# A quantised feed-forward stage: rows turned by transposing DMAs, a third double bank, two scalings on ScalarE

## The chip, the cores and the metric

The kernel runs on one core of a Trainium2 chip. The metric is device time in microseconds (us) for one execution of the whole program, and less is better. The times and the profile are of one core throughout.

## The reference, cut to what matters

One decoder layer on 16 sequences of 256 tokens and 512 features: a state-space block, a cross attention block and a feed-forward block, each followed by a layer normalisation without weights. Only the last block is touched:

```python
def _quant_weight(w):                      # ternary weights
    scale = jnp.clip(jnp.mean(jnp.abs(w)), EPS, None)
    wq = jnp.clip(jnp.round(w / scale), -1.0, 1.0) * scale
def _quant_act(x):                         # 8 bits, one scale for each row
    scale = 127.0 / jnp.clip(jnp.max(jnp.abs(x), axis=-1, keepdims=True), EPS, None)
    xq = jnp.clip(jnp.round(x * scale), -128.0, 127.0) / scale
def bitlinear(x, w):
    return jnp.einsum('btc,oc->bto', _quant_act(x), _quant_weight(w))
h = bitlinear(x, w_gate_up)                # 512 -> 2 * 2048
a, b = jnp.split(h, 2, axis=-1)
h = jax.nn.silu(a) * b
return bitlinear(h, w_down)                # 2048 -> 512
...
x = _layernorm(x + _L0_ffn_ref(x, L0_ffn_w_gate_up, L0_ffn_w_down), axis=-1)
```

The input of this block is itself the layer normalisation of what the attention stage leaves.

## The kernel before

The program has three stages, one after another: `state_space_phase`, `cross_attention_phase` and `feed_forward_phase`. They are separate blocks, so the order of work in the third does not reach into the other two. The weights of the feed-forward block arrive as ternary bf16 values in DRAM (`w_tern`), the rows as `x2`.

`feed_forward_phase` handles the 4096 rows in 32 tiles of 128 rows. The loop is written out in full: every engine runs `body(t, ...)` for t from −2 to 33, and its instructions stand in the order of `body`. An engine takes its own instructions strictly in that order; between engines there are only semaphores. In step t the engines work on several tiles:

- **tile t+2**: `x2r` (the raw rows) is normalised. VectorE takes statistics (`a_stats`, `a_mv`), GpSimd raises the variance to the power −0.5 (`a_rs`, L1934), VectorE writes `x2n` (L2012) and its largest absolute value `amax` (L2022).
- **tile t+1**: `xq` is `x2n` times 127 / max plus a large constant (`MAGIC`), which rounds to an integer (VectorE, L1986). ScalarE takes the constant off again and writes bf16, `xqb` (L1908). TensorE transposes its 4 blocks of 128x128 into `tra_ps` (L1874), and ScalarE copies them to `xqT` (L1916).
- **tile t**: four chunks c of 512 columns. TensorE computes gate and up products with 8 matmuls of 512 columns for each chunk (L1863) into one of two double banks `gu_ps`. ScalarE takes SiLU of the gate half into `sa` (L1899), VectorE multiplies by the up half into `hh` (`gate_up(c)`, L1959) and takes the largest absolute value into `hmax` (`largest(c)`, L1966).
- **tile t−1**: VectorE takes the maximum over the four chunks (L1972) and works out `factor` and `deq` (L1974 to L1981), one pair for this tile's `hh` and tile t+1's `x2n`. ScalarE scales `hh` in place (L1903), and later writes the rounded bf16 `hq` (L1913). TensorE transposes 16 blocks into `trc_ps` (L1881), and ScalarE copies them to `hqT` (L1921).
- **tile t−2**: 16 matmuls with `hqT` for the second product into `dn_ps` (`second_product`, L1849). VectorE adds the rows (`yo`, L2003), takes statistics (`c_stats`, L2008, `c_mv`, L2017), GpSimd makes `c_rs` (L1937), VectorE normalises `yo` (L2026), and SP stores it (L1831).

The order on each engine within a step, by hand:

- TensorE: chunk 0, second product, chunks 1 to 3, transposes of `xqb`, transposes of `hq`;
- ScalarE: SiLU 0, scale `hh`, `xqb`, SiLU 1, `hq`, SiLU 2, SiLU 3, `xqT`, `hqT`;
- VectorE: `factor`, `xq`, `gate_up(0)`, statistics of x, `largest(0)`, aggregate, `gate_up(1)`, `yo`, `largest(1)`, statistics of `yo`, `gate_up(2)`, `x2n`, `largest(2)`, aggregate of `yo`, `amax`, `gate_up(3)`, last normalisation, `largest(3)`.

PSUM has 8 banks of 512 float32 columns. Before, four hold `gu_ps`, two `trc_ps`, one `tra_ps` and one `dn_ps`. SP issues every DMA of the stage. At the start it issues two of the four loads of gate and up weights, 1 MB each, ahead of its loop, the other two in the first step, behind a wait for the first tile's normalisation, and the 2 MB of `dn` in the second step.

## Time and profile before

| | us |
|---|---|
| runs, median of 3 | 3519.32 (3518.9 to 3521.92) |
| profiled execution, its own time | 3514.81 |
| profiled execution, span | 3513.0 |
| of it the feed-forward stage, from its first DMA at 3100.9 | 412 |

The span runs from the first to the last instruction in the trace of one execution. TensorE is named PE in the profile, its weight loads PEld, VectorE DVE, ScalarE ACT, GpSimd POOL; SP issues DMAs. "L1863" is line 1863 of the kernel before. Times are microseconds, if not marked ns. An idle time in square brackets or behind a bar is that of the engine ahead of the instruction, with what ended it. Matmuls are pipelined, so their busy time can overlap the next one's.

### The profile page before, as it was taken

The page shows a single profiled execution, that of the slowest core. Times are in us where ns is not written, and L with a number is a line of the kernel's source. Part 1 is how long each engine was busy: PE and PEld are TensorE (multiplying, and loading weights), DVE is VectorE, ACT ScalarE, POOL GpSimd, SP SyncE. Part 2 cuts the span into 40 slices and gives each one's busy share as a digit, 9 for nine tenths or more (in the row PEclk, how much of TensorE's full clock was granted, in tenths as well). Part 3 has the DMA queues.
Part 4 walks back from the last instruction along what each step waited for, and adds up shares of the span by engine and source line. Part 5 has one row for each costly group of instructions (what it writes and reads, how often), then busy time and mean ns, then how long its engine had stood idle before and what let it go on. Part 6 is the DMA issues. An engine that isn't in the chain of part 4 may idle for free. (4 is left out here: it accounts for less than half of the span.)

```text
span 3513.0 us, 47488 instructions
## 1 busy us (share of the span) xinstructions
PE 3082.0 (88%) x16134; PEld 1815.3 (52%) x16134; DVE 2915.0 (83%) x2878; ACT 2567.4 (73%) x4981; POOL 2268.3 (65%) x1426
## 2 busy tenths in 40 slices
PE   7788888888888888888887579999999999979998
PEld 5566566656665666566665333433443443334444
...
GB/s 162 22 46 76 70 7 76 73 65 15 75 73 54 27 75 73 27 52 76 70 19 96 112 135 151 175 156 167 162 159 180 176 133 169 57 122 43 44 48 34
DMA packets 164386, 311.93 MB, mean 89 GB/s; under 512 B 22737, under 2 KB 80209, under 8 KB 164001
## 3 DMA queue, kind: packets, MB, share of 16 engines
...
## 5 line engine op out<-in xcount | busy, mean ns | idle before, releaser
L875 POOL TENSOR_TENSOR bu<-du,bc 128x1024 f32<-128x1024 f32 x512 | 1197.7, 2365 | 59.4 <-DVE dt L362 33.9
L963 DVE TENSOR_TENSOR_SCAN states<-states,bu 128x1024 f32<-128x1024 f32 x448 | 1026.8, 2292 | 119.0 <-ACT states L742 67.7
L742 ACT ACTIVATE states<-dt,negA 128x256 f32<-128x256 f32 x2048 | 850.5, 462 | 336.0 <-DVE hc L976 315.5
L1615 DVE TENSOR_REDUCE mmax<-s_ps 128x2 f32<-128x1024 f32 x512 | 624.7, 1224 | 249.2 <-PE s_ps L1334 232.5
L1459 ACT ACTIVATE pt<-s_ps 128x512 f32<-128x512 f32 x1024 | 572.7, 596 | 332.7 <-PE s_ps L1343 323.3
L542 PE MATMUL y_ps<-id_sb,hc 128*128 128x128 f32 x3584 | 490.0, 281 | 155.7 <-DVE hc L976 155.7
L976 DVE TENSOR_TENSOR hc<-states,bc 128x1024 f32<-128x1024 f32 x448 | 548.4, 1224 | 49.8 <-DMA bc<-bc_scratch 2.2
L542 PEld LDWEIGHTS y_ps<-id_sb,hc 128*128 128x128 f32 x3584 | 414.3, 144 | 318.9 <-DVE hc L976 282.5
L1343 PE MATMUL s_ps<-qst,kst 105*128 105x512 bf16 x1024 | 379.5, 386 | 12.0 <-ACT pt L1459 5.1
L1334 PE MATMUL s_ps<-kst,qst 102*128 102x512 bf16 x1024 | 317.6, 393 | 56.5 <-DMA kst<-mask_d 46.4
L507 PE MATMUL proj<-xpad,diagW 128*128 128x256 f32 x960 | 242.1, 384 | 54.7 <-ACT xpad L680 49.2
L1354 PE MATMUL pv_ps<-pt,vaug 128*32 128x512 f32 x2048 | 276.3, 613 | 12.5 <-ACT o_sb L1500 11.9
L502 PE MATMUL proj<-xT_sb,win_sb 128*128 128x256 f32 x1024 | 261.3, 385 | 16.5 <-DMA win_sb<-in_w_in 7.1
L504 PE MATMUL proj<-win_sb,xT_sb 128*128 128x512 f32 x512 | 244.9, 598 | 8.4 <-ACT u L682 8.4
L1863 PE MATMUL gu_ps<-gu,xqT 128*128 128x512 bf16 x1024 | 235.0, 383 | 8.9 <-ACT xqT L1916 6.3
L519 PE MATMUL proj<-wout_sb,y 128*128 128x512 f32 x512 | 241.9, 602 | 0.7 <-ACT y L692 0.7
L1334 PEld LDWEIGHTS s_ps<-kst,qst 102*128 102x128 bf16 x1024 | 79.1, 99 | 304.5 <-DVE mmax L1615 202.3
L507 PEld LDWEIGHTS proj<-xpad,diagW 128*128 128x128 f32 x960 | 172.0, 190 | 88.2 <-issue 29.4
L502 PEld LDWEIGHTS proj<-xT_sb,win_sb 128*128 128x128 f32 x1024 | 186.3, 193 | 41.3 <-ACT xpad L680 10.9
L1343 PEld LDWEIGHTS s_ps<-qst,kst 105*128 105x128 bf16 x1024 | 100.7, 99 | 167.1 <-ACT pt L1459 99.7
L1863 PEld LDWEIGHTS gu_ps<-gu,xqT 128*128 128x128 bf16 x1024 | 95.5, 98 | 133.3 <-DVE hh L1959 14.1
L883 POOL TENSOR_TENSOR hp<-hp,bc 128x1024 f32<-128x1024 f32 x64 | 151.5, 2368 | 0.0
...
## 6 DMA issues: line engine op xcount, KB each, us to landing
bc<-bc_scratch SPq DMA_DIRECT2D x128, 512.0 KB, 5.2
...
x<-xres SPq DMA_DIRECT2D x31, 512.0 KB, 7.1
...
xT_sb<-in_xT SPq DMA_DIRECT2D x16, 512.0 KB, 3.3
```

What stands on the lines that cost most here:

```text
L502: m = pe.matmul(proj[:, 0:SEQ], win_sb[:, k, 0, i * P:(i + 1) * P], xT_sb[:, k, :], start=start, stop=stop)
L507: m = pe.matmul(proj[:, 0:SEQ], diagW[:, i, k, :], xpad[:, i % 2, k:k + SEQ], start=start, stop=stop)
L542: m = pe.matmul(y_ps[:, i, :], src[:, n * SEQ + i * P:n * SEQ + (i + 1) * P], id_sb[:, :], start=False, stop=(c == CPT - 1 and n == NS - 1 ...
L742: a = act.activation(states[:, bank, first:first + SEQ], dt[:, t, :], ACT.Exp, scale=negA[:, t, c * NS + n:c * NS + n + 1])
L875: pool.tensor_tensor(bu[:, buf, :].rearrange("p (n l) -> p n l", n=NS), du[:, t % (2 * GRP):t % (2 * GRP) + 1, :].to_broadcast([P, NS, SEQ ...
L963: m = dve.tensor_tensor_scan(dst, src, bu[:, BU_OF[k][0], half * 2 * SEQ:(half + n) * 2 * SEQ], 0.0, ALU.mult, ALU.add)
L976: m = dve.tensor_tensor(hc[:, i % 2, cols], states[:, bank:bank + n, :].rearrange("p i l -> p (i l)"), bc[:, c, 1, cols], ALU.mult)
L1334: m = pe.matmul(s1_ps[:, pair, i, :], qst[0:ROWS1, par, u, tt * P:(tt + 1) * P], kst[0:ROWS1, par, u, :], start=True, stop=True)
L1343: pe.matmul(s2_ps[:, st % 2, :], kst[0:ROWS2, par, u, st * P:(st + 1) * P], qst[0:ROWS2, par, u, :], start=True, stop=True).then_inc(s2_re ...
L1459: act.activation(pt[:, g % 2, u % HG, st, :], s2_ps[:, st % 2], ACT.Exp).then_inc(exp_done, 1)
L1615: dve.tensor_reduce(mmax[:, u // HG, c:c + 2], s1_ps[:, pair], AX.X, ALU.max).then_inc(s1_free, 1)
L1863: mm = pe.matmul(gu_ps[:, c % 2, side, :], xqT[:, slot % 2, k, :], gu[:, c, side, k, :], start=(k == 0), stop=(k == HK - 1))
```

## The change

It touches the feed-forward stage alone.

- The transposes on TensorE, their identity, the PSUM tiles `tra_ps` and `trc_ps`, and ScalarE's two copies are gone. SP issues two transposing DMAs for each tile, from `xqb` to `xqT` and from `hq` to `hqT` (now with two buffers). ScalarE waits for the end of a transposing DMA before it writes its source again.
- `gu_ps` has three double banks (`RING`) instead of two. The second product follows chunk 1 instead of chunk 0.
- `xq` and the last normalisation of `yo` are computed on ScalarE (`Identity` with scale and bias). For the latter GpSimd makes `c_shift` as well, and both small additions of EPS are on GpSimd.
- ScalarE's order in a step is SiLU 0, `xq`, scale `hh`, `xqb`, `hq`, SiLU 1, SiLU 2, normalise `yo`, SiLU 3. VectorE's is `factor`, `gate_up(0)`, statistics of x, `largest(0)`, aggregate, `gate_up(1)`, `largest(1)`, `x2n`, `yo`, `gate_up(2)`, statistics of `yo`, `largest(2)`, aggregate of `yo`, `amax`, `gate_up(3)`, `largest(3)`.
- `x2r` has two buffers, `x2n` five, and rows are loaded four tiles ahead. The third and fourth load of gate and up weights no longer stand behind a wait.

```diff
-def feed_forward_phase(nc, x2, w_tern, w_scales, ident_bf, out):
+RING = 3
+
+
+def feed_forward_phase(nc, x2, w_tern, w_scales, out):
...
-        x2r = sb("x2r", [P, HID])
-        x2n = sb("x2n", [P, 4, HID])
+        x2r = sb("x2r", [P, 2, HID])
+        x2n = sb("x2n", [P, 5, HID])
-        hqT = sb("hqT", [P, FK, P], BF16)
+        hqT = sb("hqT", [P, 2, FK, P], BF16)
...
-        gu_ps = ps("gu_ps", [P, 2, 2, CH])
-        trc_ps = ps("trc_ps", [P, FK, P], BF16)
-        tra_ps = ps("tra_ps", [P, 2 * HK, P], BF16)
+        c_shift = sb("c_shift", [P, 1])
+
+        gu_ps = ps("gu_ps", [P, RING, 2, CH])
         dn_ps = ps("dn_ps", [P, HID])
...
+        def bank(t, c):
+            return (t * CHUNKS + c) % RING
...
+            load_rows(1)
+
+            def body(t, par):
+                if t == -2:
                     load_gu(2)
                     load_gu(3)
-                if isinstance(t, int) and t == -1:
+                if active(t + 1):
+
+                    sp.wait_ge(xq_ready, t + 2)
+                    if active(t - 1):
+                        sp.wait_ge(gu_mm, t * CHUNKS)
+                    sp.dma_start_transpose(xqT[:, 1 - par, :, :], xqb[:, :]).then_inc(xqT_in, 16)
+                if t == -1:
                     load_dn()
+                if active(t + 4):
+                    sp.wait_ge(a_loaded_use, t + 3)
+                    load_rows(t + 4)
+                if active(t - 1):
+
+                    sp.wait_ge(hq_ready, t)
+                    if active(t - 3):
+                        sp.wait_ge(dn_mm, t - 2)
+                    sp.dma_start_transpose(hqT[:, 1 - par, :, :], hq[:, :]).then_inc(hqT_in, 16)
                 if active(t - 2):
-                    wait(y_ready, t - 1)
-                    sp.dma_start(rows(out, t - 2), yo[:, slot % 2, :]).then_inc(y_out[slot % 2], 16)
-
-            run(sp, body)
+                    sp.wait_ge(y_ready, t - 1)
+                    sp.dma_start(rows(out, t - 2), yo[:, par, :]).then_inc(y_out[par], 16)
...
-                pe.wait_ge(hqT_ready, t - 1)
-                if isinstance(t, int) and t == 2:
+
+            def second_product(t, par):
+
+                pe.wait_ge(hqT_in, (t - 1) * 16)
+                if t == 2:
                     pe.wait_ge(dn_in, 16)
                 if active(t - 3):
                     pe.wait_ge(dn_read, t - 2)
                 for k in range(FK):
-                    mm = pe.matmul(dn_ps[:, :], hqT[:, k, :], dn[:, k, :], start=(k == 0), stop=(k == FK - 1))
+                    mm = pe.matmul(dn_ps[:, :], hqT[:, par, k, :], dn[:, k, :], start=(k == 0), stop=(k == FK - 1))
                 mm.then_inc(dn_mm, 1)
 
-            def body(t, slot, stores):
+            def body(t, par):
                 for c in range(CHUNKS):
                     if active(t):
                         if c == 0:
-                            pe.wait_ge(xqT_ready, t + 1)
-                        if not (isinstance(t, int) and t == 0 and c < 2):
-                            pe.wait_ge(h_done, t * CHUNKS + c - 1)
-                        if isinstance(t, int) and t == 0:
+                            pe.wait_ge(xqT_in, (t + 1) * 16)
+                        if t * CHUNKS + c >= RING:
+                            pe.wait_ge(h_done, t * CHUNKS + c + 1 - RING)
+                        if t == 0:
                             pe.wait_ge(gu_in[c], 16)
                         for side in range(2):
                             for k in range(HK):
-                                mm = pe.matmul(gu_ps[:, c % 2, side, :], xqT[:, slot % 2, k, :],
+                                mm = pe.matmul(gu_ps[:, bank(t, c), side, :], xqT[:, par, k, :],
                                                gu[:, c, side, k, :],
                                                start=(k == 0), stop=(k == HK - 1))
                         mm.then_inc(gu_mm, 1)
-                    if c == 0 and active(t - 2):
-                        second_product(t)
-                if active(t + 1):
-                    pe.wait_ge(xq_ready, t + 2)
-                    if not (isinstance(t, int) and t == -1):
-                        pe.wait_ge(xqT_ready, t + 1)
-                    for k in range(HK):
-                        mm = pe.transpose(tra_ps[:, k, :], xqb[:, k * P:(k + 1) * P], idb[:, :])
-                    mm.then_inc(tra_mm, 1)
-                if active(t - 1):
-                    pe.wait_ge(hq_ready, t)
-                    if not (isinstance(t, int) and t == 1):
-                        pe.wait_ge(hqT_ready, t - 1)
-                    for k in range(FK):
-                        mm = pe.transpose(trc_ps[:, k, :], hq[:, k * P:(k + 1) * P], idb[:, :])
-                    mm.then_inc(trc_mm, 1)
-
-            run(pe, body)
+                    if c == 1 and active(t - 2):
+                        second_product(t, par)
+
+            run(body)
...
-            def body(t, slot, stores):
-                par = slot % 2
+            def body(t, par):
                 h = hh[:, 1 - par, :]
-                for c in range(CHUNKS):
+
+                def silu(c):
                     if active(t):
                         act.wait_ge(gu_mm, t * CHUNKS + c + 1)
-                        if not (isinstance(t, int) and t == 0 and c < 2):
+                        if t * CHUNKS + c >= 2:
                             act.wait_ge(h_done, t * CHUNKS + c - 1)
-                        act.activation(sa[:, c % 2, :], gu_ps[:, c % 2, 0, :], ACT.Silu,
+                        act.activation(sa[:, c % 2, :], gu_ps[:, bank(t, c), 0, :], ACT.Silu,
                                        scale=deq[:, par, 0:1]).then_inc(silu_done, 1)
-                    if c == 0 and active(t - 1):
-                        act.wait_ge(scales, t + 2)
-                        act.activation(h, h, ACT.Identity, bias=magic[:, :], scale=factor[:, 1:2])
-                    if c == 0 and active(t + 1):
-                        act.wait_ge(xq_shift, t + 2)
-                        if not (isinstance(t, int) and t == -1):
-                            act.wait_ge(tra_mm, t + 1)
-                        act.activation(xqb[:, :], xq[:, :], ACT.Copy, bias=-MAGIC).then_inc(xq_ready, 1)
-                    if c == 1 and active(t - 1):
-                        act.drain()
-                        if not (isinstance(t, int) and t == 1):
-                            act.wait_ge(trc_mm, t - 1)
-                        act.activation(hq[:, :], h, ACT.Copy, bias=-MAGIC).then_inc(hq_ready, 1)
+
+                silu(0)
                 if active(t + 1):
-                    act.wait_ge(tra_mm, t + 2)
-                    act.activation(xqT[:, 1 - par, :, :], tra_ps[:, 0:HK, :], ACT.Copy).then_inc(xqT_ready, 1)
+                    act.wait_ge(scales, t + 2)
+                    act.activation(xq[:, :], x2n[:, (t + 1) % 5, :], ACT.Identity, bias=magic[:, :], scale=factor[:, 0:1])
                 if active(t - 1):
-                    act.wait_ge(trc_mm, t)
-                    if not (isinstance(t, int) and t == 1):
-                        act.wait_ge(dn_mm, t - 1)
-                    act.activation(hqT[:, :, :], trc_ps[:, :, :], ACT.Copy).then_inc(hqT_ready, 1)
-
-            run(act, body)
+                    act.wait_ge(scales, t + 2)
+                    act.activation(h, h, ACT.Identity, bias=magic[:, :], scale=factor[:, 1:2])
+                if active(t + 1):
+                    act.drain()
+                    if t >= 0:
+                        act.wait_ge(xqT_in, (t + 1) * 16)
+                    act.activation(xqb[:, :], xq[:, :], ACT.Copy, bias=-MAGIC).then_inc(xq_ready, 1)
+                if active(t - 1):
+                    act.drain()
+                    if active(t - 2):
+                        act.wait_ge(hqT_in, (t - 1) * 16)
+                    act.activation(hq[:, :], h, ACT.Copy, bias=-MAGIC).then_inc(hq_ready, 1)
+                silu(1)
+                silu(2)
+                if active(t - 2):
+
+                    act.wait_ge(c_rstd, t - 1)
+                    act.activation(yo[:, par, :], yo[:, par, :], ACT.Identity, bias=c_shift[:, :],
+                                   scale=c_rs[:, :]).then_inc(y_ready, 1)
+                silu(3)
+
+            run(body)
...
                     pool.wait_ge(a_var, t + 3)
+                    pool.tensor_scalar(a_ve[:, :], a_mv[:, 1:2], EPS, None, ALU.add)
+                    pool.drain()
                     pool.tensor_tensor(a_rs[:, :], a_ve[:, :], half_neg[:, :], ALU.pow).then_inc(a_rstd, 1)
                 if active(t - 2):
                     pool.wait_ge(c_var, t - 1)
-                    pool.tensor_tensor(c_rs[:, :], c_ve[:, :], half_neg[:, :], ALU.pow).then_inc(c_rstd, 1)
-
-            run(pool, body)
+                    if active(t - 3):
+                        pool.wait_ge(y_ready, t - 2)
+                    pool.tensor_scalar(c_ve[:, :], c_mv[:, 1:2], EPS, None, ALU.add)
+                    pool.drain()
+                    pool.tensor_tensor(c_rs[:, :], c_ve[:, :], half_neg[:, :], ALU.pow)
+                    pool.drain()
+                    pool.tensor_scalar(c_shift[:, :], c_mv[:, 0:1], c_rs[:, :], -1.0,
+                                       ALU.mult, ALU.mult).then_inc(c_rstd, 1)
...
+                    if t >= 0:
+                        dve.wait_ge(xq_ready, min(t + 1, TILES))
                     dve.tensor_scalar(factor[:, :], small[:, 1, :], QMAX, None, ALU.mult).then_inc(scales, 1)
-                if active(t + 1):
-                    dve.wait_ge(scales, t + 2)
-                    if not (isinstance(t, int) and t == -1):
-                        dve.wait_ge(xq_ready, t + 1)
-                    dve.tensor_scalar(xq[:, :], x2n[:, (slot + 1) % 4, :], factor[:, 0:1], MAGIC,
-                                      ALU.mult, ALU.add).then_inc(xq_shift, 1)
                 gate_up(0)
                 if active(t + 2):
-                    dve.wait_ge(x2r_in, (t + 3) * 16)
-                    dve.bn_stats(a_stats[:, :], x2r[:, :])
+                    dve.wait_ge(x2r_in[par], ((t + 2) // 2 + 1) * 16)
+                    dve.bn_stats(a_stats[:, :], x2r[:, par, :])
                 largest(0)
                 if active(t + 2):
                     dve.drain()
-                    dve.bn_aggr(a_mv[:, :], a_stats[:, :])
-                    dve.drain()
-                    dve.tensor_scalar(a_ve[:, :], a_mv[:, 1:2], EPS, None, ALU.add).then_inc(a_var, 1)
+                    dve.bn_aggr(a_mv[:, :], a_stats[:, :]).then_inc(a_var, 1)
                 gate_up(1)
+                largest(1)
+                if active(t + 2):
+                    dve.wait_ge(a_rstd, t + 3)
+                    dve.tensor_scalar(x2n[:, (t + 2) % 5, :], x2r[:, par, :], a_mv[:, 0:1], a_rs[:, :],
+                                      ALU.subtract, ALU.mult).then_inc(a_loaded_use, 1)
                 if active(t - 2):
                     dve.wait_ge(dn_mm, t - 1)
-                    if not (isinstance(t, int) and t < 4):
-                        dve.wait_ge(y_out[par], stores * 16)
-                    dve.scalar_tensor_tensor(y, dn_ps[:, :], deq[:, par, 1:2], x2n[:, (slot + 2) % 4, :],
+                    if t >= 4:
+                        dve.wait_ge(y_out[par], (t // 2 - 1) * 16)
+                    dve.scalar_tensor_tensor(y, dn_ps[:, :], deq[:, par, 1:2], x2n[:, (t - 2) % 5, :],
                                              ALU.mult, ALU.add).then_inc(dn_read, 1)
-                largest(1)
+                gate_up(2)
                 if active(t - 2):
                     dve.wait_ge(dn_read, t - 1)
                     dve.bn_stats(c_stats[:, :], y)
-                gate_up(2)
-                if active(t + 2):
-                    dve.wait_ge(a_rstd, t + 3)
-                    dve.tensor_scalar(x2n[:, (slot + 2) % 4, :], x2r[:, :], a_mv[:, 0:1], a_rs[:, :],
-                                      ALU.subtract, ALU.mult).then_inc(a_loaded_use, 1)
                 largest(2)
                 if active(t - 2):
                     dve.drain()
-                    dve.bn_aggr(c_mv[:, :], c_stats[:, :])
-                    dve.drain()
-                    dve.tensor_scalar(c_ve[:, :], c_mv[:, 1:2], EPS, None, ALU.add).then_inc(c_var, 1)
+                    if active(t - 3):
+                        dve.wait_ge(c_rstd, t - 2)
+                    dve.bn_aggr(c_mv[:, :], c_stats[:, :]).then_inc(c_var, 1)
                 if active(t + 2):
                     dve.wait_ge(a_loaded_use, t + 3)
-                    dve.tensor_reduce(amax[:, 0:1], x2n[:, (slot + 2) % 4, :], AX.X, ALU.max, apply_absolute_value=True)
+                    dve.tensor_reduce(amax[:, 0:1], x2n[:, (t + 2) % 5, :], AX.X, ALU.max, apply_absolute_value=True)
                 gate_up(3)
-                if active(t - 2):
-                    dve.wait_ge(c_rstd, t - 1)
-                    dve.tensor_scalar(y, y, c_mv[:, 0:1], c_rs[:, :], ALU.subtract, ALU.mult).then_inc(y_ready, 1)
                 largest(3)
```

## Rows read from the trace of the kernel before

**Rows 1.** Busy time by stretch: us, busy and instructions by engine, clock, DMA share, GB/s.

```profile
3200.00:3490.00 290.00, 286.37 (x1662) 137.84 (x1660) 249.92 (x573) 230.13 (x219) 25.84 (x47) 1.00 0.13 43
```

**Rows 2.** The chain that ended last, one tile: start us, us, what.

```profile
3205.01 1.90 PE gu_ps L1863 x8
3206.91 3.55 PE dn_ps L1849 x16
3210.46 5.21 PE gu_ps L1863 x24
...
3216.92 0.39 PE gu_ps L1863
```

**Rows 3.** Waits from 3130 to 3490 us: total us, times, longest.

```profile
ACT hh L1903 <- DVE factor L1981: 49.6, 30, 2.2
```

**Rows 4.** ScalarE in order of time over the same tile: start us, us, what.

```profile
3209.57 2.09 ACT L1903 ACTIVATE hh<-hh,magic,factor 128x2048 f32<-128x2048 f32 x1 [1.93 <-DVE factor L1981]
3211.57 0.61 ACT L1908 ACTIVATE xqb<-xq 128x512 bf16<-128x512 f32 x1
3212.22 0.69 ACT L1899 ACTIVATE sa<-gu_ps,deq 128x512 f32<-128x512 f32 x1
3212.99 1.91 ACT L1913 ACTIVATE hq<-hh 128x2048 bf16<-128x2048 f32 x1
3214.81 0.67 ACT L1899 ACTIVATE sa<-gu_ps,deq 128x512 f32<-128x512 f32 x1
...
3221.16 2.09 ACT L1903 ACTIVATE hh<-hh,magic,factor 128x2048 f32<-128x2048 f32 x1 [1.61 <-DVE factor L1981]
```

**Rows 5.** VectorE in order of time over the same tile.

```profile
3212.94 0.75 DVE L1959 SCALAR_TENSOR_TENSOR hh<-gu_ps,deq,sa 128x512 f32<-128x512 f32 x1 [0.56 <-ACT sa L1899]
3213.61 0.74 DVE L2003 SCALAR_TENSOR_TENSOR yo<-dn_ps,deq,x2n 128x512 f32<-128x512 f32 x1
3214.27 0.68 DVE L1966 TENSOR_REDUCE hmax<-hh 128x1 f32<-128x512 f32 x1
3214.86 0.69 DVE L2008 BATCH_NORM_STATS2 c_stats<-yo 128x6 f32<-128x512 f32 x1
3215.51 0.75 DVE L1959 SCALAR_TENSOR_TENSOR hh<-gu_ps,deq,sa 128x512 f32<-128x512 f32 x1
3216.18 0.54 DVE L2012 TENSOR_SCALAR x2n<-x2r,a_mv,a_rs 128x512 f32<-128x512 f32 x1
3216.63 0.68 DVE L1966 TENSOR_REDUCE hmax<-hh 128x1 f32<-128x512 f32 x1
3217.38 0.18 DVE L2017 BATCH_NORM_AGGREGATE c_mv<-c_stats 128x2 f32<-128x6 f32 x1
...
3219.42 0.68 DVE L1966 TENSOR_REDUCE hmax<-hh 128x1 f32<-128x512 f32 x1
```

**Rows 6.** GpSimd's groups by shape: busy us, mean ns, idle us before them.

```profile
L352 POOL TENSOR_TENSOR sp_m<-sp_m,sp_t 128x512 f32<-128x512 f32 x63 | 80.2, 1273 | 9.3 <-issue 0.4
...
L1937 POOL TENSOR_TENSOR c_rs<-c_ve,half_neg 128x1 f32<-128x1 f32 x32 | 17.6, 550 | 183.7 <-DVE c_ve L2019 183.7
...
L914 POOL TENSOR_TENSOR w_sum<-w_sum,w_piece 128x3 f32<-128x3 f32 x16 | 3.2, 198 | 0.0
```

**Rows 7.** DMA issues of the whole span: KB each, median us to landing.

```profile
xT_sb<-in_xT SPq DMA_DIRECT2D x16, 512.0 KB, 3.3
...
idb<-in_ident_bf SPq DMA_DIRECT2D x1, 32.0 KB, 1.6
```

**Rows 8.** DMA queue from 1580 to 1590 us: packets, MB, share of 16 engines.

```profile
q1 hardware_dynamic: 48, 0.03, 1.2%
```

**Rows 9.** The same queue from 3130 to 3490 us.

```profile
q1 hardware_dynamic: 8208, 14.95, 12.4%
```

**Rows 10.** Busy time by stretch, at the end of the span, columns as in rows 1.

```profile
3500.00:3506.00 6.00, 4.07 (x11) 1.54 (x12) 0.00 (x0) 1.87 (x1) 0.00 (x0) 0.54 0.12 44
```

**Rows 11.** Busy time by stretch, at the start of the stage, columns as in rows 1.

```profile
3103.00:3111.00 8.00, 0.58 (x4) 0.35 (x4) 3.52 (x12) 1.17 (x2) 0.58 (x1) 0.50 1.02 369
```

55 lines of the change are left out of this document (20 added, 35 removed).

## The prediction

> **What bounds the kernel now.** I read the views in this order: the table of busy time by stretch, the chain of work that ended last, the order of time on ScalarE and on VectorE over one tile, the waits, and last the DMA rows. Only the feed-forward stage changes, which is the last 412 us of the 3513 us span. Everything ahead of it stays as it is.
>
> In the long even stretch TensorE is busy 286 of 290 us at the full clock, while VectorE and ScalarE show 86% and 79% [rows 1]. That looks like a plain TensorE bound, and the chain agrees: it runs from product to product [rows 2], and one tile of 128 rows takes 3216.92 − 3205.01 = 11.91 us. In it 48 products of 512 columns take 1.90 + 3.55 + 5.21 = 10.66 us. The other 1.25 us are the 20 transposes and the copy to SBUF that they wait for.
>
> The reader should now look at what lies just under this bound. ScalarE waits for VectorE's `factor` once in every tile [rows 3], and VectorE's `hh` of chunk 1 waits for ScalarE's SiLU of chunk 1 [rows 5]. These two waits close a loop. `factor` releases the scaling of `hh`, behind which SiLU 1 stands in ScalarE's order. SiLU 1 releases `hh` 1. Behind `hh` 1, in VectorE's order, stands everything up to the next `factor`, because that needs the maximum over all four chunks. Its two legs can be read off directly:
>
> - ScalarE's leg, from the start of the scaling at 3209.57 to `hh` 1 at 3212.94, takes 3.37 us [rows 4, 5];
> - VectorE's leg, from there to the next start of the scaling at 3221.16, takes 8.22 us [rows 4, 5].
>
> Together they take 11.59 us, which is only 0.32 us under TensorE's 11.91. So two limits lie nearly level, and an edit that shortens one and lengthens the other has to be costed on both.
>
> **TensorE's side of the change.** All 20 transposes of a tile leave TensorE, and no wait for a copy stands between two tiles any more. With 48 products in a row, a tile costs about 10.5 us (10.66 less the 0.16 by which the first eight exceed 8 × 0.217). The third double bank lets chunk c+3 start once chunk c has been read. Alone this would be worth 1.4 us a tile. TensorE doesn't get to show it, as follows.
>
> **ScalarE's leg after.** The new order is SiLU 0, scale `x2n` into `xq`, scale `hh`, write `xqb`, write `hq`, and only then SiLU 1. Start to start [rows 4]:
>
> - the scaling of x, 128x512. It is not in the trace on this engine. Nearest is `xqb`, of the same size: its 0.61 us. Bounds 0.52 (a quarter of the 2.09 for 2048 columns) and 0.69 (SiLU);
> - the scaling of `hh`: 2.00, plus 0.10 for the drain that now follows;
> - `xqb`: 0.65, plus 0.08 for a drain;
> - `hq`: 3214.81 − 3212.99 = 1.82. Before, this stood behind SiLU 1 and lay beside VectorE's work. Now VectorE's `hh` 1 waits behind it;
> - SiLU 1 to `hh` 1: 0.72.
>
> The sum is 5.98 us, against 3.37. VectorE has only `hh` 0, the statistics of x and the maximum of chunk 0 to do meanwhile, and then stands.
>
> **VectorE's leg after.** Start to start [rows 5]. `hh` 1 is now followed directly by its own maximum, so it counts with its whole 0.75 plus 0.03 to release (as SiLU 1's end at 3212.91 releases `hh` at 3212.94): 0.78. Then maximum 0.59, `x2n` 0.45, `yo` 0.66, `hh` 2 0.67, statistics of `yo` 0.65, maximum and drain 0.75, aggregate 0.18 and 0.08 to release. GpSimd hears of the variance 4.81 us after `hh` 1.
>
> Here the second part of the change strikes. The last normalisation moves to ScalarE, and there it stands **ahead of SiLU 3**. It needs GpSimd's `c_rstd` of the same step of the loop. Before, nobody but the normalisation itself waited for that. What is late next is SiLU 3, then `hh` 3, its maximum, and `factor`. In detail:
>
> - GpSimd: add, drain, power, drain, multiply. The power takes 0.55; a sum of 3 columns took 0.20; a drain leaves some 0.15 (9.3 us over 63) [rows 6]. That is 0.20 + 0.15 + 0.55 + 0.15 + 0.20 = 1.25 us. Below, the power and the two drains alone are 0.85; above, it could be 1.95, if each small operation costs as much as the power. I take 1.25, since the small ones are simple arithmetic like the sum;
> - ScalarE: release 0.05, the normalisation 0.65, SiLU 3 0.72;
> - VectorE: `hh` 3 0.78, then from its maximum to the next scaling 3221.16 − 3219.42 = 1.74.
>
> The leg is 4.81 + 1.25 + 0.05 + 0.65 + 0.72 + 0.78 + 1.74 = 10.00 us, against 8.22. What leaves VectorE doesn't pay for this: `xq` and the small addition for x were not in this leg at all, and the last normalisation and the other addition are less than the 2.67 us from GpSimd's start to the end of SiLU 3, under which only `amax` lies.
>
> Loop: 5.98 + 10.00 = **15.98 us a tile**, 4.07 more than now. For the 30 steps in which all parts are active: 122 us.
>
> **The transposing DMAs.** Nothing in the trace transposes by DMA. The `hqT` transfer moves 512 KB, `xqT` 128 KB. Fastest is a plain transfer of the size: 512 KB landed in 3.3 us. Slowest is the price of a single 128x128 block, 32 KB that landed in 1.6 us, paid 16 times one after another: 25.6 us, and 6.4 for `xqT` [rows 7]. Between them: a transposed block has runs of no more than 128 × 2 = 256 bytes, so 2048 and 512 pieces. Packets of 1 KB and less took 1.2% of 16 × 10 us over 48, which is 40 ns each [rows 8]; those of the stage, mostly 2 KB, took 87 ns [rows 9]. At 40 ns on 16 engines the pieces take 5.1 and 1.3 us. With 1.5 us to start and land I take 6.6 and 2.8.
>
> The cover for that is wide, thanks to the longer loop. `xqb` is ready 3.4 us after the scaling starts, and SiLU 0 of the next tile is not wanted before some 13.5. Less the 1.9 us of the product, 8 us are free. `hq` is ready at 5.4, but on SP's queue `hqT` stands behind the load of rows, which waits for this step's `x2n`; that ends at 5.98 + 0.78 + 0.59 + 0.54 = 7.9. Behind `hqT` stands the store, which waits for `yo` until 12.7 anyway, and then the next `xqT`, not wanted before 19.4. The product must have begun by about 18.2, so that chunk 2 is there when VectorE wants `hh` 2 a loop later: 10.3 us are free. Both transfers cost nothing at these values. The Trainium skill speaks against the move: "VectorE: DVE Perf Modes", sections "The three transpose paths" and "Rules for kernel authors", gives a 128x128 bf16 block 390 ns on TensorE and 1309 ns by DMA, and advises TensorE where the result may land in PSUM. By that, as an estimate, 20 blocks one after another would be 26.2 us a tile. "Advanced Engine Details and Errata", section "X-Bar Transpose (TRN2)", has such DMAs at 350 to 400 GB/s, which would be 1.4 us for `hqT`. No row here can decide between them.
>
> TensorE's clock: idle for about 4 us a tile it may fall, as at the end of the trace, where 0.54 was granted on average after a gap [rows 10]. Two chunks at half the clock are 3.5 us more, within a slack of some 6 (chunk 2 would end 17.0 us after the scaling starts and is wanted at 23.5).
>
> **Start and end.** The loads of gate and up are now all issued before the first `xqT` and stand ahead of it in the same queue: 4.6 MB at 369 GB/s is 12 us [rows 11], so it lands near 3117 instead of 3111. The step in which `hq` first appears costs some 1 us more too, and the first tiles lie partly under the load, so I take 6 us for the start (3 to 12). At the end the 6.6 us of `hqT` stand where 16 transposes and a copy of 2048 columns stood, by my estimate 3.6 together, and GpSimd and ScalarE take 1 us more: 4 us (1 to 24).
>
> **Sum.** 122 + 6 + 4 = 132 us. Against the profiled execution's own time of 3514.8 this gives 3647. The median of the runs shown lies 4.5 above that execution: 3651 us, 3.7% slower.
>
> **Rivals and chances.**
>
> - *Forecast, the loop of ScalarE, VectorE and GpSimd decides*, 15.4 to 16.8 us a tile: 3625 to 3700. Chance 0.70.
> - *The transposing DMAs decide.* It happens if `hqT` takes more than 10.3 us to land. `hq` may also not be rewritten before its transfer has read it. At the slow bound each tile costs 25.6 + 6.4 = 32 us, 20.1 more: 3519 + 31 × 20.1 + 20 = 4160. For it: no row shows such a transfer and small pieces are dear. Against: large transfers here use all engines. Chance 0.22, spread from 3700 up. The first of the two rules above would end here, at some 4000 by 26.2 us a tile.
> - *The normalisation hardly delays SiLU 3*, because GpSimd's part is shorter or ScalarE and VectorE overlap more: the leg loses up to 2.1 us, 13.8 a tile, 3590. Chance 0.04.
> - *TensorE stays the bound* (the other side). Place: between `factor` and `hh` 1. If my legs count time in which these engines in truth waited for TensorE, so that the new loop is under 11.9 us, the tile costs 10.5 and the stage gains 31 × 1.4 = 43 us, less 10 at both ends: 3486. It needs 4 us of error in rows between which hardly any idle time lies. Chance 0.04.
>
> So the time lies between 3600 and 3760 with about 8 in 10, where the upper end takes in an `hqT` of up to some 14 us. A change under 0.2%, 7 us, can't be told from none. Faster 0.03, same 0.01, slower 0.96.
>
> **What would show it.** In the profile after: a tile of about 16 us; TensorE busy about two thirds; ScalarE's `yo` waiting for GpSimd's `c_shift` in each tile; VectorE's `hh` waiting for SiLU some 3.5 us before chunk 1 and 2 before chunk 3; waits of `factor` as now. Wrong would be: TensorE's products waiting for `hqT` by DMA in every tile, or `hq` waiting for it; or no wait of `yo` at all. The prediction fails if `hqT` takes over 10 us, or if ScalarE's order turns out not to hold SiLU 1 back.

## The result and the profile after

| | median us | runs, us | profiled execution, us | its span, us | feed-forward stage, us |
|---|---|---|---|---|---|
| before | 3519.11 | 4, 3517.03 to 3521.92 | 3514.81 | 3513.0 | 412.1 |
| after | 3664.74 | 4, 3660.15 to 3668.15 | 3668.15 | 3666.4 | 550.8 |

The change makes the kernel slower: the ratio is 1.0413, with a 95% interval of 1.0398 to 1.0428. The forecast was 3651 us, with a range of 3600 to 3760.

The stage column runs from the stage's first DMA to the end of the span: 3513.0 − 3100.9 before and 3666.4 − 3115.6 after. The stage grew by 138.7 us. The other 14.7 us lie ahead of it, in code that the change doesn't touch, and the section on the prediction comes back to them.

The table of busy time by stretch, of the kernel after:

```profile
3200.00:3600.00 400.00, 298.16 (x1190) 118.93 (x1188) 230.25 (x494) 206.50 (x221) 44.78 (x123) 0.92 0.32 73
```

TensorE is now busy 75% of the stretch, against 99% before [rows 1], and its mean granted clock falls from 1.00 to 0.92. VectorE is at 58% and ScalarE at 52%. No engine is the bound by its share. The waits of the same stretch (us in total, times, longest) say what is:

```profile
DVE hh L1964 <- ACT sa L1891: 154.3, 49, 4.0
...
ACT yo L1916 <- POOL c_shift L1942: 140.9, 25, 5.9
...
PE gu_ps L1869 <- DVE hh L1964: 61.8, 31, 3.6
ACT xq L1897 <- DVE factor L1988: 52.1, 25, 2.4
...
PE dn_ps L1855 <- DMA hqT<-hq: 39.9, 24, 3.3
```

25 tiles lie in it. VectorE waits twice a tile for SiLU, ScalarE once for GpSimd and once for `factor`. Three engines hand the work round, and each stands while another has it. TensorE waits too, 31 times for `hh` and 24 times for `hqT`, in nearly every tile. The same view has no row in which ScalarE or VectorE waits for TensorE, so nothing stands behind these waits of TensorE. The order of time of one tile, from one scaling to the next, shows both legs (start us, us, what):

```profile
3304.66 0.81 ACT L1897 ACTIVATE xq<-x2n,magic,factor 128x512 f32<-128x512 f32 x1 [2.06 <-DVE factor L1988]
3305.38 2.08 ACT L1900 ACTIVATE hh<-hh,magic,factor 128x2048 f32<-128x2048 f32 x1
3307.52 0.63 ACT L1905 ACTIVATE xqb<-xq 128x512 bf16<-128x512 f32 x1
...
3308.23 1.91 ACT L1910 ACTIVATE hq<-hh 128x2048 bf16<-128x2048 f32 x1
3310.05 1.25 ACT L1891 ACTIVATE sa<-gu_ps,deq 128x512 f32<-128x512 f32 x2
3310.75 0.75 DVE L1964 SCALAR_TENSOR_TENSOR hh<-gu_ps,deq,sa 128x512 f32<-128x512 f32 x1 [4.00 <-ACT sa L1891]
...
3313.13 3.26 SPq L1835 DMA_TRANSPOSE hqT<-hq  x1
...
3315.52 0.22 POOL L1938 TENSOR_SCALAR c_ve<-c_mv 128x1 f32<-128x1 f32 x1 [7.76 <-DVE c_mv L2018]
3315.89 0.56 POOL L1940 TENSOR_TENSOR c_rs<-c_ve,half_neg 128x1 f32<-128x1 f32 x1
3316.62 0.26 POOL L1942 TENSOR_SCALAR c_shift<-c_mv,c_rs 128x1 f32<-128x1 f32 x1 [0.17 <-issue]
3316.92 0.81 ACT L1916 ACTIVATE yo<-yo,c_shift,c_rs 128x512 f32<-128x512 f32 x1 [5.62 <-POOL c_shift L1942]
3317.64 1.25 ACT L1891 ACTIVATE sa<-gu_ps,deq 128x512 f32<-128x512 f32 x2
3318.34 0.75 DVE L1964 SCALAR_TENSOR_TENSOR hh<-gu_ps,deq,sa 128x512 f32<-128x512 f32 x1 [2.33 <-ACT sa L1891]
3318.46 3.63 PE L1855 MATMUL dn_ps<-dn,hqT 128*128 128x512 bf16 x16 [2.51 <-DMA hqT<-hq]
...
3320.93 0.81 ACT L1897 ACTIVATE xq<-x2n,magic,factor 128x512 f32<-128x512 f32 x1 [2.06 <-DVE factor L1988]
```

The loop goes round in 3320.93 − 3304.66 = 16.27 us. The first leg, from the scaling to `hh` 1 at 3310.75, takes 6.09 us. VectorE has stood for the last 4.00 of them. The second leg takes 10.18. In it `yo` starts at 3316.92, after ScalarE has idled for 5.62 us, and SiLU 3, `hh` 3 and `factor` follow behind. The mean over 17 tiles from 3191 to 3469 us is 16.32, and 15 of the 17 take 16.28 or 16.29.

The DMA issues of the stretch, with the median time from issue to landing, and the first product of the stage:

```profile
hqT<-hq SPq DMA_TRANSPOSE x25, 4.6
xqT<-xqb SPq DMA_TRANSPOSE x24, 2.5
```

```profile
3124.41 1.31 SPq L1824 DMA_TRANSPOSE xqT<-xqb  x1
...
3132.32 3.17 PE L1869 MATMUL gu_ps<-gu,xqT 128*128 128x512 bf16 x7 [20.62 <-DMA xqT<-xqb]
```

### The profile page after: what moved, and what is told of

It is laid out like the page before. It is cut to its first block and busy times, and to the rows that moved or that the text cites. A ratio compares the mean times of both kernels' runs of the same rounds, so it can differ in the third digit from the quotient of the medians.

```text
span 3666.4 us, 46268 instructions
## 1 busy us (share of the span) xinstructions
PE 3094.9 (84%) x15494; PEld 1788.2 (49%) x15494; DVE 2881.3 (79%) x2750; ACT 2534.7 (69%) x4981; POOL 2289.8 (62%) x1522
## 5 line engine op out<-in xcount | busy, mean ns | idle before, releaser
L1334 PE MATMUL s_ps<-kst,qst 102*128 102x512 bf16 x1024 | 321.5, 397 | 70.1 <-DMA kst<-mask_d 61.1
L1869 PE MATMUL gu_ps<-gu,xqT 128*128 128x512 bf16 x1024 | 263.9, 415 | 100.1 <-DVE hh L1964 79.4
L1964 DVE SCALAR_TENSOR_TENSOR hh<-gu_ps,deq,sa 128x512 f32<-128x512 f32 x128 | 95.8, 749 | 202.2 <-ACT sa L1891 201.9
L1869 PEld LDWEIGHTS gu_ps<-gu,xqT 128*128 128x128 bf16 x1024 | 104.0, 105 | 255.1 <-DMA xqT<-xqb 105.2
```

The source lines that it names most:

```text
L1334: m = pe.matmul(s1_ps[:, pair, i, :], qst[0:ROWS1, par, u, tt * P:(tt + 1) * P], kst[0:ROWS1, par, u, :], start=True, stop=True)
L1869: mm = pe.matmul(gu_ps[:, bank(t, c), side, :], xqT[:, par, k, :], gu[:, c, side, k, :], start=(k == 0), stop=(k == HK - 1))
```

## The experiments

All variants compute everything, in another order or on another engine. The stage and the mean tile are from the profiled execution of each, the tile from the first to the last scaling of `hh` between about 3180 and 3478 us. The ratio is to the runs of the kernel before that were made beside it.

| kernel | median us | ratio, 95% interval | stage us | mean tile us |
|---|---|---|---|---|
| before | 3519.11 | | 412.1 | 11.92 |
| after | 3664.74 | 1.0413, 1.0398 to 1.0428 | 550.8 | 16.32 |
| 1, normalisation behind SiLU 3 | 3588.97 | 1.0212, 1.0190 to 1.0233 | 477.3 | 13.96 |
| 2, `hq` behind SiLU 1 | 3599.27 | 1.0245, 1.0222 to 1.0268 | 492.9 | 14.38 |
| 3, both | 3537.39 | 1.0058, 1.0038 to 1.0078 | 429.7 | 12.35 |
| 4, `hqT` transferred twice | 3657.36 | 1.0406, 1.0383 to 1.0428 | 552.8 | 16.39 |
| 5, DMAs and banks alone | 3552.31 | 1.0091, 1.0076 to 1.0107 | 442.9 | 12.90 |
| 6, new order of ScalarE | 3555.41 | 1.0099, 1.0085 to 1.0114 | 449.7 | 13.03 |
| 7, 6 with a late weight load | 3555.30 | 1.0097, 1.0083 to 1.0111 | 438.4 | 12.72 |
| 8, 6 with `hq` ahead of SiLU 2 | 3504.32 | 0.9949, 0.9930 to 0.9968 | 398.6 | 11.41 |
| 9, `hq` early, `hqT` ahead of the rows | 3502.00 | 0.9947, 0.9930 to 0.9963 | 397.4 | 11.21 |
| 10, before with `xqT` by DMA | 3506.21 | 0.9974, 0.9958 to 0.9989 | 401.4 | 11.45 |

The mean hides two kinds of tile in some of these kernels. In the third most tiles take 11.94 us and 5 of 23 take 13.4 to 13.8, in the eighth 11.06 with 3 of 25 at 13.4 to 13.7, in the ninth 11.05 with 2 of 25 at 13.2, in the sixth 12.1 to 12.8 with 7 of 22 at 14.2 to 14.5. In these longer tiles the granted clock is 0.87 to 0.88 instead of 1.00. Two neighbouring tiles of the sixth kernel by stretch (columns as in rows 1), and the second product of the longer one, which takes 5.31 us instead of 3.63:

```profile
3289.64:3303.83 14.19, 12.17 (x47) 5.04 (x48) 9.91 (x22) 7.75 (x9) 1.83 (x5) 0.88 0.36 86
3303.83:3316.28 12.45, 10.48 (x47) 4.62 (x48) 9.91 (x22) 7.75 (x9) 1.83 (x5) 1.00 0.39 95
```

```profile
3290.76 5.31 PE L1855 MATMUL dn_ps<-dn,hqT 128*128 128x512 bf16 x16 [1.97 <-DMA hqT<-hq]
```

So where a mean lies above the sum of the legs, it comes from such tiles, and a stage time moves by 1.5 to 2.6 us with each.

**1. Only the normalisation moves back**, behind SiLU 3:

```diff
                 silu(2)
+                silu(3)
                 if active(t - 2):
                     act.wait_ge(c_rstd, t - 1)
                     act.activation(yo[:, par, :], ...)
-                silu(3)
```

> The changed kernel with one move: on ScalarE the last normalisation stands behind SiLU 3 instead of ahead of it. Theory (a loop of ScalarE and VectorE decides, 6.09 + 10.18 = 16.27 us a tile as read from the profile after): SiLU 3 no longer waits for GpSimd, VectorE's leg falls from 10.18 to about 7.8, a tile takes 13.9 us and the whole 3665 - 30 x 2.4 = 3593 us. Rival, the transposing DMAs or TensorE decide: nothing changes, 3665.

**2. Only `hq` moves**, from ahead of SiLU 1 to behind it:

```diff
+                silu(1)
                 if active(t - 1):
                     act.drain()
...
                     act.activation(hq[:, :], h, ACT.Copy, bias=-MAGIC).then_inc(hq_ready, 1)
-                silu(1)
                 silu(2)
```

> The changed kernel with another single move: on ScalarE hq is written behind SiLU 1 instead of ahead of it. Loop theory: ScalarE's leg falls from 6.09 to about 4.2, SiLU 2 comes some 0.15 later, a tile takes 14.6 us, the whole 3665 - 30 x 1.7 = 3614. Rival (DMAs or TensorE decide): 3665.

**3. Both moves**, the two diffs above together.

> Both moves of the two other kernels together. Loop theory: the two savings add up, as they lie in different legs: about 12.2 us a tile, 3665 - 30 x 4.1 = 3542. If another limit (DMA, TensorE at a lower clock) lies between, the sum falls short: at 13 us a tile 3567.

The measured medians are 3588.97, 3599.27 and 3537.39 us. The first and the third lie 4 to 5 us below what was expected. The second lies 15 below its 3614: the tile takes 14.38 us in place of the expected 14.6, and 7.6 us of the difference in the medians are not in the stage. The first move shortens the mean tile by 2.36 us and the second by 1.94. The order of time of the first, from scaling to `hh` 1 to scaling:

```profile
3303.73 0.81 ACT L1897 ACTIVATE xq<-x2n,magic,factor 128x512 f32<-128x512 f32 x1 [0.21 <-DVE factor L1988]
...
3309.83 0.75 DVE L1964 SCALAR_TENSOR_TENSOR hh<-gu_ps,deq,sa 128x512 f32<-128x512 f32 x1 [4.01 <-ACT sa L1891]
...
3316.00 0.81 ACT L1917 ACTIVATE yo<-yo,c_shift,c_rs 128x512 f32<-128x512 f32 x1 [4.63 <-POOL c_shift L1942]
...
3317.59 0.81 ACT L1897 ACTIVATE xq<-x2n,magic,factor 128x512 f32<-128x512 f32 x1 [0.21 <-DVE factor L1988]
```

`yo` still waits 4.63 us for GpSimd, but nobody stands behind it any more. The first leg is 6.10 us as in the kernel after; the second is 7.76 in place of 10.18. The second kernel is the mirror image: its first leg is 3308.34 − 3304.23 = 4.11 us, its second 3318.60 − 3308.34 = 10.26. With both moves:

```profile
3312.45 0.81 ACT L1897 ACTIVATE xq<-x2n,magic,factor 128x512 f32<-128x512 f32 x1 [0.21 <-DVE factor L1988]
3316.55 0.75 DVE L1964 SCALAR_TENSOR_TENSOR hh<-gu_ps,deq,sa 128x512 f32<-128x512 f32 x1 [2.02 <-ACT sa L1891]
...
3324.39 0.81 ACT L1897 ACTIVATE xq<-x2n,magic,factor 128x512 f32<-128x512 f32 x1 [0.21 <-DVE factor L1988]
```

The legs are 4.10 and 7.84 us, 11.94 together. The loop of the prediction is shown: each leg can be shortened alone by a change in order, with no work taken away, and the stage gives back 73.5 and 57.9 us for them singly and 121.1 of the 138.7 for both. That 121.1 is less than 73.5 + 57.9 = 131.4 comes from the longer tiles. In the usual tile the moves add up: 16.28 falls by 2.42 to 13.86, by 1.91 to 14.37, and by 4.34 to 11.94.

**4. The rival, the transposing DMAs decide.** Each `hqT` transfer is issued twice, the second time into a tile that nobody reads, and `hq` may be rewritten only when both have landed:

```diff
                     sp.dma_start_transpose(hqT[:, 1 - par, :, :], hq[:, :]).then_inc(hqT_in, 16)
+                    if active(t - 2):
+                        sp.wait_ge(hqT2_in, (t - 1) * 16)
+                    sp.dma_start_transpose(hqT2[:, :, :], hq[:, :]).then_inc(hqT2_in, 16)
...
                     if active(t - 2):
                         act.wait_ge(hqT_in, (t - 1) * 16)
+                        act.wait_ge(hqT2_in, (t - 1) * 16)
```

> The changed kernel with the transposing DMA of hq made twice, the second time into a tile that nobody reads, and hq is rewritten only after both. Loop theory: the transfers are covered, no change, 3660 to 3675. Rival, the transposing DMAs set the pace: 4.6 us more a tile (the time to landing in the profile after), 3665 + 138 = 3800.

Measured: 3657.36 us, and the intervals of its ratio and of the kernel after overlap. The tile of 16.39 us is 0.07 longer. The DMA issues show twice as many transfers at the same time to land:

```profile
hqT<-hq SPq DMA_TRANSPOSE x50, 4.5
```

So the load on the queue and the rewriting of `hq` don't set the time of the kernel after. The first copy lands no later here, so this run doesn't test its latency. That is tested by experiments 1 to 3, in which the transfers stay and the tile falls by up to 4.3 us.

**5. The DMAs, the third double bank and the second row buffer alone.** Both scalings, the small additions and the orders of ScalarE and VectorE are those of before. On ScalarE:

```diff
-                    act.activation(xq[:, :], x2n[:, (t + 1) % 5, :], ...)
...
+                silu(1)
                 if active(t - 1):
                     act.drain()
...
-                silu(1)
                 silu(2)
-                if active(t - 2):
-                    act.wait_ge(c_rstd, t - 1)
-                    act.activation(yo[:, par, :], ...)
                 silu(3)
```

> Only one part of the change: transposing DMAs, three double banks and the two buffers for the rows, while xq, the last normalisation and the small additions stay where they were before, in the orders of before on ScalarE and VectorE. Loop theory: the legs of before, 3.37 + 8.22 = 11.6 us a tile instead of TensorE's 11.91, so 9 us gained and about as much lost at start and end: 3519, between 3510 and 3528. Rival, before TensorE's transposes alone set the pace: 10.5 us a tile, 3519 - 42 + 9 = 3486.

Measured: 3552.31 us. **Both the theory and its rival missed.** Two waits show where to look:

```profile
ACT sa L1891 <- PE gu_ps L1869: 66.7, 58, 3.1
...
PE dn_ps L1855 <- DMA hqT<-hq: 37.2, 19, 2.9
```

ScalarE waits for TensorE, and TensorE for the DMA. The order of time:

```profile
3308.92 3.63 PE L1855 MATMUL dn_ps<-dn,hqT 128*128 128x512 bf16 x16 [1.95 <-DMA hqT<-hq]
...
3314.31 0.69 ACT L1891 ACTIVATE sa<-gu_ps,deq 128x512 f32<-128x512 f32 x1 [0.87 <-PE gu_ps L1869]
3315.03 0.75 DVE L1947 SCALAR_TENSOR_TENSOR hh<-gu_ps,deq,sa 128x512 f32<-128x512 f32 x1 [0.50 <-ACT sa L1891]
3315.70 0.54 DVE L2000 TENSOR_SCALAR x2n<-x2r,a_mv,a_rs 128x512 f32<-128x512 f32 x1
...
3316.26 0.33 SPq L1796 DMA_DIRECT2D x2r<-x  x1
...
3317.02 3.30 SPq L1835 DMA_TRANSPOSE hqT<-hq  x1
...
3322.30 5.31 PE L1855 MATMUL dn_ps<-dn,hqT 128*128 128x512 bf16 x16 [2.85 <-DMA hqT<-hq]
```

That is a loop of its own, through TensorE, ScalarE, VectorE, SP's queue and the transfer. The second product (3.46 us) stands ahead of chunk 2 on TensorE (1.93), that releases SiLU 2 (0.72), `hh` 2 (0.67) and `x2n` (0.56). `x2n` releases the load of rows, ahead of `hqT` on SP's queue (0.76), and `hqT` takes 5.28 us until the next second product starts. The sum is 13.38, the distance from 3308.92 to 3322.30. This is a long turn: the two before it, between the second products at 3284.03, 3296.43 and 3308.92, take 12.40 and 12.49 us, and the mean of 12.90 holds 6 of 23 tiles at 14.2 to 14.7.

**6. A new order of ScalarE** to open both loops of the prediction: SiLU 0, scale `hh`, SiLU 1, `xqb`, SiLU 2, `hq`, SiLU 3, normalisation. The scaling of x goes back to VectorE:

```diff
                     act.activation(h, h, ACT.Identity, bias=magic[:, :], scale=factor[:, 1:2])
+                silu(1)
...
+                silu(2)
                 if active(t - 1):
                     act.drain()
...
-                silu(1)
-                silu(2)
+                silu(3)
                 if active(t - 2):
                     act.wait_ge(c_rstd, t - 1)
                     act.activation(yo[:, par, :], ...)
-                silu(3)
```

> The changed kernel with another order on ScalarE: SiLU 0, scale hh, SiLU 1, xqb, SiLU 2, hq, SiLU 3, last normalisation, and xq back on VectorE. Loop theory: ScalarE's leg is 2.0 + 0.1 + 0.7 = 2.8 us, VectorE's 7.8, together 10.6, level with TensorE's 48 products at 10.5; with some friction 10.8 us a tile, 3519 - 30 x 1.1 + 9 = 3495, between 3485 and 3508: faster than both kernels. Rival, moving work to a DMA and to GpSimd cannot gain here because the latencies of DMA and GpSimd stay on the path: 3519 or more.

**7. The same, with the last load of gate and up issued behind the first `xqT`** :

```diff
                 if t == -2:
                     load_gu(2)
-                    load_gu(3)
...
                 if t == -1:
+                    load_gu(3)
                     load_dn()
```

> The kernel with the other order on ScalarE, and the last of the four loads of gate and up weights issued behind the first transposing DMA instead of ahead of it. If the first xqT stands in the queue behind the loads (7.9 us from issue to TensorE's first product in the profile after), it lands 2 to 4 us earlier: 2 to 4 us below the kernel without this. If the wait has another cause: the same.

Measured: 3555.41 and 3555.30 us; the sixth misses by 60. The order of time of the sixth:

```profile
3298.61 1.91 ACT L1909 ACTIVATE hq<-hh 128x2048 bf16<-128x2048 f32 x1
3300.54 1.78 SPq L1835 DMA_TRANSPOSE hqT<-hq  x1
...
3304.90 3.63 PE L1855 MATMUL dn_ps<-dn,hqT 128*128 128x512 bf16 x16 [1.92 <-DMA hqT<-hq]
3308.36 7.07 PE L1869 MATMUL gu_ps<-gu,xqT 128*128 128x512 bf16 x31
...
3310.29 0.69 ACT L1891 ACTIVATE sa<-gu_ps,deq 128x512 f32<-128x512 f32 x1 [3.27 <-PE gu_ps L1869]
...
3311.06 1.91 ACT L1909 ACTIVATE hq<-hh 128x2048 bf16<-128x2048 f32 x1
```

It is the loop of experiment 5 by another way. `hq` now stands behind SiLU 2, and SiLU 2 needs chunk 2, which TensorE computes behind the second product, which needs `hqT` of the tile before. The steps are `hq` 1.93 to the issue, 4.36 to the product, 3.46 for it, 1.93 for chunk 2 and 0.77 for SiLU 2: 12.45 us, the distance between the two `hq`. The seventh kernel leaves the median where it was. In its profile the stage's first product starts 14.1 us after the first DMA, against 16.7 in the sixth, and the first scaling of `hh` 27.5 us against 32.0. The first `xqT` did stand behind the loads. Whether this is there in total time the runs, which spread over 10 us, don't tell.

**8. The sixth with `hq` ahead of SiLU 2**, which cuts exactly that loop:

```diff
-                silu(2)
                 if active(t - 1):
                     act.drain()
...
                     act.activation(hq[:, :], h, ACT.Copy, bias=-MAGIC).then_inc(hq_ready, 1)
+                silu(2)
                 silu(3)
```

> The kernel with the other order on ScalarE (e6_order), and in it one swap: hq is written ahead of SiLU 2 instead of behind it. Theory of a third loop, read from the profile of e6_order: hq 1.91, its transposing DMA 4.4, second product 3.5, chunk 2 1.9, SiLU 2 0.7, then hq again, 12.45 us. The swap opens it, and what is left are the legs of ScalarE and VectorE, 2.8 + 8.5: about 11.5 us a tile instead of 12.7, 3555 - 35 = 3520, between 3510 and 3530. Rival, the DMA or TensorE sets 12.5 us for another reason (throughput): no change, 3555.

Measured: 3504.32 us, 51 less than the sixth for one activation moved by one place, and 0.5% faster than the kernel before. This lies below the expected 3510 to 3530; the usual tile takes 11.06 us where 11.5 were expected. `hq` is at 3303.53, 3314.59 and 3325.64: 11.06 and 11.05 us apart. The third loop is confirmed.

**9. `hq` early and `hqT` ahead of the load of rows.** The order of ScalarE is SiLU 0, scale `hh`, `xqb`, SiLU 1, `hq`, SiLU 2, SiLU 3, normalisation. On SP's queue `hqT` goes ahead of the load of rows, and the load of weights is as in 7. Against the sixth kernel:

```diff
                     act.activation(h, h, ACT.Identity, bias=magic[:, :], scale=factor[:, 1:2])
-                silu(1)
                 if active(t + 1):
...
                     act.activation(xqb[:, :], xq[:, :], ...)
-                silu(2)
+                silu(1)
                 if active(t - 1):
...
                     act.activation(hq[:, :], h, ...)
+                silu(2)
                 silu(3)
...
-                if active(t + 4):
-                    sp.wait_ge(a_loaded_use, t + 3)
-                    load_rows(t + 4)
                 if active(t - 1):
...
                     sp.dma_start_transpose(hqT[:, 1 - par, :, :], hq[:, :]).then_inc(hqT_in, 16)
+                if active(t + 4):
+                    sp.wait_ge(a_loaded_use, t + 3)
+                    load_rows(t + 4)
```

> Everything the theories of the loops suggest with both transposing DMAs kept: ScalarE in the order SiLU 0, scale hh, xqb, SiLU 1, hq, SiLU 2, SiLU 3, last normalisation; xq on VectorE; on SP the transposing DMA of hq ahead of the load of rows; the last weight load behind the first xqT. Legs 3.4 + 7.9 = 11.3 us and TensorE 10.5: 11.4 us a tile, 3519 - 15 + 5 = 3509, between 3500 and 3520. Rival, the latency of the DMA stays on the path: 12.3 us or more a tile as in the kernel with both moves, 3535.

Measured: 3502.00 us, the lowest median of all. It can't be told from the eighth. Its order of time:

```profile
3309.59 2.10 ACT L1897 ACTIVATE hh<-hh,magic,factor 128x2048 f32<-128x2048 f32 x1 [0.21 <-DVE factor L1985]
3312.81 0.75 DVE L1961 SCALAR_TENSOR_TENSOR hh<-gu_ps,deq,sa 128x512 f32<-128x512 f32 x1 [0.63 <-ACT sa L1891]
...
3319.79 3.63 PE L1855 MATMUL dn_ps<-dn,hqT 128*128 128x512 bf16 x15 [1.09 <-DMA hqT<-hq]
3320.64 2.09 ACT L1897 ACTIVATE hh<-hh,magic,factor 128x2048 f32<-128x2048 f32 x1 [0.21 <-DVE factor L1985]
```

The legs are 3.22 and 7.83 us, 11.05 together. That is the loop of the prediction in its shortest form here. In these rows TensorE still waits 1.09 us for `hqT`, but neither leg waits for TensorE, and the tile doesn't come down to the 10.5 us that its products would allow.

Two comparisons say more. ScalarE's order here is that of the third kernel without the scaling of x and the drain that came with it. The first leg falls from 4.10 to 3.22 us, the second stays (7.84 and 7.83), and the usual tile falls by 0.89: that is what this scaling costs on ScalarE, if the other order on SP's queue does nothing to it. And the eighth kernel takes the same 11.06 us although SiLU 1 comes earlier there, with legs of 2.70 and 8.35. Its VectorE waits 0.50 us for SiLU 2 ahead of `hh` 2, and `hh` 2 starts 5.79 us after the scaling in both kernels. `hq` stands ahead of SiLU 2 in both. So in the eighth the loop runs over SiLU 2 and `hh` 2, and in the ninth the way over `hh` 1 is level with it.

**10. The kernel before with x alone transposed by DMA.** `hqT` stays on TensorE. The last normalisation stands at the end of ScalarE's order, and the second product behind chunk 1:

```diff
+                if active(t + 1):
+                    wait(xq_ready, t + 2)
...
+                    sp.dma_start_transpose(xqT[:, (t + 1) % 2, :, :], xqb[:, :]).then_inc(xqT_in, 16)
...
-                    for k in range(HK):
-                        mm = pe.transpose(tra_ps[:, k, :], xqb[:, k * P:(k + 1) * P], idb[:, :])
...
+                if active(t - 2):
+                    act.wait_ge(c_rstd, t - 1)
+                    act.activation(yo[:, par, :], yo[:, par, :], ...)
```

> The kernel before with a small part of the change: only xqb is transposed by DMA (the transfer with the wide cover), hq stays on TensorE with two double banks; the last normalisation goes to ScalarE at the very end of its order; the second product follows chunk 1. TensorE 48 products and 16 transposes, 11.4 us; legs 3.4 + 7.8 = 11.2. So 11.45 us a tile instead of 11.91: 3519 - 14 = 3505, between 3497 and 3513, faster than both. Rival, the first xqT behind the weight loads and the longer order on ScalarE eat it: 3519.

Measured: 3506.21 us, 0.26% faster, as expected. TensorE is busy 247.98 of the 250 us from 3200 on, and the tile takes 11.45 us: here TensorE is still the bound, with 4 transposes fewer. This gain comes without the large transfer.

## Why the prediction was right, step by step

**The bound of before.** That a loop of ScalarE and VectorE lies just under TensorE's 11.91 us was read from the rows. The legs are measured from one scaling to the next, so their sum is the length of that one tile, and the 11.59 us are the loop's own length only because neither leg holds a wait for TensorE. Over the 24 tiles from 3178 to 3478 us the distances are 11.58 to 12.26 with a mean of 11.92, so 11.59 is among the shortest. Experiment 9 shows a loop of this kind: with TensorE relieved and the new loops avoided, the tile stops at 11.05, not at 10.5. It is shorter than 11.59 because the last normalisation (0.54 us) and an addition are gone from VectorE's leg, which takes 7.83 in place of 8.22. The loop of before itself, with nothing taken from it, was not laid open by any run; experiment 5 was meant to and met the loop through `hqT`.

**ScalarE's leg.** Predicted 5.98 us, measured 6.09. The scaling of x takes 0.72 start to start in place of 0.61. Of this leg, the 1.91 us of `hq` ahead of SiLU 1 are shown by experiment 2 (1.94 us of the tile), and the scaling of x by experiment 9 against 3 (0.88 us of the leg, with what follows it).

**VectorE's leg.** Predicted 10.00 us, measured 10.18. From `hh` 1 to GpSimd's start it took 4.77 (4.81 predicted). GpSimd's three operations, from start to the start of `yo`, took 1.40 against 1.25 + 0.05: 0.22 and 0.26 for the simple ones, 0.56 for the power, the rest drains and gaps. `yo` to SiLU 3 took 0.72 (0.65), and the last maximum to the scaling 3320.93 − 3319.12 = 1.81 (1.74). The loop's error is a mean of 16.32 against 15.98. It is made of terms that are off by a few hundredths to a tenth each, most of them low, and no step is wrong. For the 1.25 us of GpSimd the rows of before allowed 0.85 to 1.95; that the guess inside them was so close is partly luck.

**The normalisation ahead of SiLU 3** is the larger of the two new costs. Experiment 1 gives 2.36 us of the tile for it. The rival by which it hardly delays SiLU 3 is dead: SiLU 3 does start only after `yo`, and VectorE's `hh` waits 2.33 us for it. Its price was worked out well: 13.8 us a tile and 3590 us is close to what experiment 1 measured, by taking the normalisation out of the way (13.96 and 3589).

**The transfers.** `hqT` landed in 4.6 us (6.6 taken) and `xqT` in 2.5 (2.8 taken). The issue came 3313.13 − 3304.66 = 8.5 us after the scaling (7.9 predicted), and the product started at 13.8, before the 18.2 at which it would have held VectorE up.

One sign that the prediction named for being wrong did appear: TensorE's products waiting for `hqT` in every tile. They wait in 24 of 25, for 39.9 us in total. The sign was badly chosen, since the prediction itself gave TensorE a slack of some 6 us a tile, and a wait inside that slack costs nothing. What shows that it does is that neither ScalarE nor VectorE waits for TensorE, and that the tile falls with the order on ScalarE while the transfers stay.

That `hqT` would land in less than 10.3 us no row of before could say: the bounds were 3.3 and 25.6. Here the forecast was a guess with a chance beside it, and it held.

The Trainium skill's page "VectorE: DVE Perf Modes", section "The three transpose paths", has a block by DMA at 1309 ns, which by my estimate would have been 26.2 us for the 20 blocks of a tile one after another. The trace doesn't agree: the two transfers together take 7.1 us, so the blocks don't add up like that. By the rate in the Trainium skill's page "Advanced Engine Details and Errata", section "X-Bar Transpose (TRN2)", my estimate for `hqT` was 1.4 us. The trace doesn't show that either: from issue to landing it took 4.6.

What the prediction did not see is the third loop. "The cover for that is wide, thanks to the longer loop" was right for the kernel after and only for it. Once the legs are shorter, the 4.4 to 5.3 us from issue to product can belong to a loop that decides. Whether they do depends on what `hq` and its transfer stand behind: with `hq` behind SiLU 2 (experiment 6), or `hqT` behind a load of rows that itself waits for `hh` 2 (experiment 5), the tile stays at 12.1 us or more, and in experiments 8 and 9 it falls to 11.05. Experiments 5 and 6, costed with the same two bounds as the prediction, missed by 33 and 60 us for that reason.

**TensorE.** Busy three quarters where two thirds were forecast. The surplus is slower products, not more of them: the mean clock is 0.92, and the second products at 3302.79 and 3318.46 take 5.31 and 3.63 us. It stayed within the slack.

**Start and end.** First product 3132.32 − 3115.60 = 16.7 us after the stage's first DMA, against 10.2 before: 6.5 (6 predicted). From the last scaling to the end of the span 21.5 us, against 18.8: 2.7 (4 predicted).

**Sum.** The stage grew by 138.7 us, 132 were forecast. By the scalings of `hh`, 5.1 us of it lie ahead of the first one, 130.9 between the first and the last, and 2.7 behind the last; the forecast had 6, 122 and 4. So the loop was sized 9 us too short and the two ends 2 too long. The 14.7 us ahead of the stage in the two profiled executions come from a wait in the attention stage, in code that both kernels share. The waits from 2000 to 3100 us, before first and after second:

```profile
PE s_ps L1334 <- DMA kst<-mask_d: 46.4, 15, 18.7
```

```profile
PE s_ps L1334 <- DMA kst<-mask_d: 61.1, 15, 18.7
```

Over the profiles of all twelve kernels, whose code ahead of the stage is the same, that wait varies from 41.5 to 61.1 us, and the stage begins between 3090.5 and 3115.6. The total time of one kernel spreads just as far, 3485.28 to 3513.52 us over the 11 runs of experiment 9, so it looks like variation from run to run. What causes it was not tried and stays open. The medians differ by 145.6 us and the stages by 138.7, and by these profiles only the latter is the change's. Of the 13.7 us between the forecast of 3651 and the measured 3664.7, then, 6.7 are the prediction's error on the stage, and the other 7 lie ahead of it, on which the prediction had nothing to say.
